# The right factor and the band output in DRAM: row, channel, column against channel, row, column

## What is computed

```python
xn = _ln(group_norm(x))                                   # 32 channels
left  = (xn @ Wl + bl) * mask * sigmoid(xn @ Wlg + blg)   # 64 channels
right = (xn @ Wr + br) * mask * sigmoid(xn @ Wrg + brg)   # 64 channels
out_gate = sigmoid(xn @ Wog + bog)
# band: out[i, k, h] = sum over |d| <= 4 of left[i + d, i, h] * right[i + d, k, h]
out = _ln(_banded_ingoing(left, right, 4)) * out_gate
x = x + out @ Wo + bo
```

## Time and profile before

| | us |
|---|---|
| median of 3 runs (3795.11 to 3798.96) | 3797.58 |
| the profiled execution | 3818.71 |
| its span, first to last instruction | 3816.9 |
| of it the three layers | about 0 to 1842 |
| of it the fourth layer | about 1842 to 3817 |
| TensorE busy | 2963.8 (78%) |
| VectorE busy | 2530.4 (66%) |
| DMA: packets, MB | 368217, 568.38 |

### The profile page before, as it was taken

The page is one execution under the profiler, slowest core; times in us unless marked ns, Lnnn a source line. Parts: engine busy times, 40 slices in busy tenths (PEclk is TensorE's granted clock), DMA queues, the critical chain, the costliest instruction groups (busy, mean ns, idle before and its releaser), DMA issues. The chain is left out here.

```text
span 3816.9 us, 37020 instructions
## 1 busy us (share of the span) xinstructions
PE 2963.8 (78%) x10962; PEld 864.5 (23%) x10962; DVE 2530.4 (66%) x2216; ACT 1906.5 (50%) x2326; POOL 1737.7 (46%) x964
## 2 busy tenths in 40 slices
PE   2685898695799596689168888888888888888886
PEld 0122322122222122222012222222222222222221
DVE  2243355143345143334159999999999999999998
ACT  0331344241244241235077677677776676676772
POOL 0110012110012120011147888878878878878876
PEclk9796998796899697899579999999999999999998
DMA  6866741766752656664747667667667676576674
GB/s 204 49 194 186 229 118 54 29 175 194 214 151 67 7 152 216 204 185 120 129 98 169 151 154 172 150 159 170 146 164 167 143 170 161 145 169 159 144 178 109
DMA packets 368217, 568.38 MB, mean 149 GB/s; under 512 B 144552, under 2 KB 247024, under 8 KB 367088
## 3 DMA queue, kind: packets, MB, share of 16 engines
q1 hardware_dynamic: 297216, 537.94, 55.3%
q10 hardware_dynamic: 70896, 29.14, 7.7%
HBM read 421.14 MB, written 145.80 MB: 149 GB/s over the span
## 5 line engine op out<-in xcount | busy, mean ns | idle before, releaser
L483 POOL TENSOR_TENSOR m_hs<-m_hs,m_cs 128x1024 f32<-128x1024 f32 x512 | 1205.6, 2360 | 347.4 <-DVE m_hs L457 347.4
L457 DVE TENSOR_TENSOR_SCAN m_hs<-m_da,m_pb 128x1024 f32<-128x1024 f32 x512 | 1170.9, 2287 | 33.2 <-ACT m_da L409 6.5
L303 PE MATMUL m_pb<-m_dtx,m_spread 64*128 64x512 f32 x2048 | 600.5, 652 | 219.0 <-DVE m_hs L457 218.4
L409 ACT ACTIVATE m_da<-m_dtb,m_a_neg 128x1020 f32<-128x1020 f32 x512 | 579.4, 1143 | 290.1 <-DMA m_dtb<-dt_rows 215.8
L452 DVE TENSOR_TENSOR m_pb<-m_pb,m_bs 128x1024 f32<-128x1024 f32 x512 | 620.6, 1212 | 34.9 <-PE m_pb L303 34.3
L1317 POOL TENSOR_TENSOR t_xc<-t_xc,t_xn 128x512 f32<-128x512 f32 x96 | 121.4, 1265 | 1112.2 <-DVE t_xn L1271 1112.2
L286 PE MATMUL m_py<-m_hs,m_gather 128*64 128x512 f32 x2048 | 566.6, 632 | 59.5 <-POOL m_hs L483 59.4
L1258 DVE TENSOR_TENSOR t_vwin<-t_bank,t_mask_k 128x512 f32<-128x512 f32 x204 | 140.4, 691 | 397.8 <-PE t_bank L968 274.3
L1314 POOL TENSOR_TENSOR t_sq<-t_xn 128x512 f32<-128x512 f32 x96 | 99.7, 1039 | 504.7 <-ACT t_xn L1163 504.7
L968 PE MATMUL t_bank<-t_rwin,t_lwin 128*128 128x256 f32 x816 | 244.7, 438 | 92.1 <-DVE t_vwin L1258 72.3
L303 PEld LDWEIGHTS m_pb<-m_dtx,m_spread 64*128 64x128 f32 x2048 | 168.2, 189 | 619.3 <-DVE m_hs L457 544.5
(11 more groups left out here) (144 smaller groups left out, 3649.0 us busy)
## 6 DMA issues: line engine op xcount, KB each, us to landing
m_dtb<-dt_rows SPq DMA_DIRECT2D x512, 512.0 KB, 6.1
right_factor<-t_tile SPq DMA_DIRECT2D x384, 128.0 KB, 2.7
t_rwin<-right_factor SPq DMA_DIRECT2D x96, 512.0 KB, 6.2
t_tile<-band_out SPq DMA_DIRECT2D x384, 128.0 KB, 3.0
t_lwin<-band_factor SPq DMA_DIRECT2D x96, 272.0 KB, 4.2
band_out<-t_vwin SPq DMA_DIRECT2D x48, 496.0 KB
band_out<-t_vwin SPq DMA_DIRECT2D x48, 480.0 KB
dt_rows<-m_dt ACTq DMA_DIRECT2D x64, 256.0 KB, 3.3
```

The costliest lines, as they stand in the source:

```text
L303: m = nc.tensor.matmul(pb[s % 2][:, half(n)], spread[rows, dg, :], dtx[par][rows, half(q)], start=True, stop=True)
L409: nc.scalar.activation(da[:, s % DA_RING, :, 1:T], dtb[s % DTB_RING][:, :].rearrange("p (r t) -> p r t", t=T)[:, :, 1:T], ACT.Exp, scale=a ...
L457: nc.vector.tensor_tensor_scan(hs[:, s % H_RING, :], da[:, s % DA_RING, :, :].rearrange("p r t -> p (r t)"), pb[s % 2][:, :], 0.0, ALU.mul ...
L483: nc.gpsimd.tensor_tensor(hs[:, s % H_RING, :], hs[:, s % H_RING, :], cs[q][:, :], ALU.mult).then_inc(hc_ready, 1)
```

## The change

`r_dram` and `v_dram` are declared as (channel, row, column) in place of (row, channel, column), and each DMA that touches them is written for it. What is computed, the order of all work, the waits and the sizes of all transfers stay the same. One channel's two image rows lie side by side now, so stores of L806 and loads of L830 are one piece of 2 KB a partition where they were two of 1 KB. Four channels of one row lie 256 KB apart now, so window loads and stores are four pieces of 1 KB a partition where they were one of 4 KB.

```diff
--- before.py
+++ after.py
@@ -803,9 +803,8 @@
                         slot = at[l, "r", n, p]
                         for hs in range(2):
                             row = first_row(n, 2 * p + (hs ^ n % 2))
-                            sp.dma_start(r_dram[row:row + 2, :, :].rearrange("r h k -> h r k"),
-                                         tile[HID * hs:HID * hs + HID, slot, :].rearrange("h (r k) -> h r k", r=2)
-                                         ).then_inc(tile_stored[slot], 16)
+                            sp.dma_start(r_dram[:, row:row + 2, :].rearrange("h r k -> h (r k)"),
+                                         tile[HID * hs:HID * hs + HID, slot, :]).then_inc(tile_stored[slot], 16)
 
                 def right_stored(l, n):
                     for slot in range(T_RING):
@@ -827,8 +826,8 @@
                         tile_free(sp, key)
                         for hs in range(2):
                             row = first_row(n, 2 * p + (hs ^ p))
-                            sp.dma_start(tile[HID * hs:HID * hs + HID, slot, :].rearrange("h (r k) -> h r k", r=2),
-                                         v_dram[row:row + 2, :, :].rearrange("r h k -> h r k")).then_inc(tile_loaded[slot], 16)
+                            sp.dma_start(tile[HID * hs:HID * hs + HID, slot, :],
+                                         v_dram[:, row:row + 2, :].rearrange("h r k -> h (r k)")).then_inc(tile_loaded[slot], 16)
 
                 def load_window(l, q):
                     slot = at[l, "chunk", q]
@@ -845,8 +844,8 @@
                         row = w_ * WIN_B
                         sp.dma_start(lwin[:, slot, :], band_dram[w_, :, HC * hc:HC * hc + HC, :].rearrange("j h i -> j (h i)")
                                      ).then_inc(win_loaded[slot], 16)
-                        sp.dma_start(rwin[:, slot, :], r_dram[row:row + P, HC * hc:HC * hc + HC, :].rearrange("j h k -> j (h k)")
-                                     ).then_inc(win_loaded[slot], 16)
+                        sp.dma_start(rwin[:, slot, :].rearrange("j (h k) -> j h k", h=HC),
+                                     r_dram[HC * hc:HC * hc + HC, row:row + P, :].rearrange("h j k -> j h k")).then_inc(win_loaded[slot], 16)
                     else:
                         c0 = HC * (q - 32)
                         for c in range(HC):
@@ -854,9 +853,8 @@
                             sp.dma_start(lwin[:, slot, o:o + P].rearrange("p (h i) -> p h i", h=8),
                                          corner_dram[:, c0 + c, :, BAND:BAND + 16]).then_inc(win_loaded[slot], 16)
                         for hg in range(8):
-                            sp.dma_start(rwin[16 * hg:16 * hg + 16, slot, :],
-                                         r_dram[ROW_C:ROWS, 8 * hg + c0:8 * hg + c0 + HC, :].rearrange("j h k -> j (h k)")
-                                         ).then_inc(win_loaded[slot], 16)
+                            sp.dma_start(rwin[16 * hg:16 * hg + 16, slot, :].rearrange("j (h k) -> j h k", h=HC),
+                                         r_dram[8 * hg + c0:8 * hg + c0 + HC, ROW_C:ROWS, :].rearrange("h j k -> j h k")).then_inc(win_loaded[slot], 16)
 
                 def store_window(l, q):
                     slot = at[l, "chunk", q]
@@ -867,13 +865,13 @@
                         w_, hc = divmod(q, 16)
                         lo, hi = (0, P - BAND) if w_ == 0 else (BAND, P - BAND)
                         row = w_ * WIN_B
-                        sp.dma_start(v_dram[row + lo:row + hi, HC * hc:HC * hc + HC, :].rearrange("j h k -> j (h k)"),
-                                     vwin[lo:hi, slot, :]).then_inc(win_stored[slot], 16)
+                        sp.dma_start(v_dram[HC * hc:HC * hc + HC, row + lo:row + hi, :].rearrange("h j k -> j h k"),
+                                     vwin[lo:hi, slot, :].rearrange("j (h k) -> j h k", h=HC)).then_inc(win_stored[slot], 16)
                     else:
                         c0 = HC * (q - 32)
                         for hg in range(8):
-                            sp.dma_start(v_dram[ROW_C + BAND:ROWS, 8 * hg + c0:8 * hg + c0 + HC, :].rearrange("j h k -> j (h k)"),
-                                         vwin[16 * hg + BAND:16 * hg + 16, slot, :]).then_inc(win_stored[slot], 16)
+                            sp.dma_start(v_dram[8 * hg + c0:8 * hg + c0 + HC, ROW_C + BAND:ROWS, :].rearrange("h j k -> j h k"),
+                                         vwin[16 * hg + BAND:16 * hg + 16, slot, :].rearrange("j (h k) -> j h k", h=HC)).then_inc(win_stored[slot], 16)
 
                 def store_x(n):
                     sp.wait_ge(x_done, 2 * UNITS * (LAYERS - 1) + n + 1)
@@ -1403,8 +1401,8 @@
          for n, t in arrays.items()}
     band_dram = nc.dram_tensor("band_factor", (2, P, HID, LROW), F32, kind="Internal").ap()
     corner_dram = nc.dram_tensor("corner_factor", (P, 8, 8, 24), F32, kind="Internal").ap()
-    r_dram = nc.dram_tensor("right_factor", (ROWS, HID, COLS), F32, kind="Internal").ap()
-    v_dram = nc.dram_tensor("band_out", (ROWS, HID, COLS), F32, kind="Internal").ap()
+    r_dram = nc.dram_tensor("right_factor", (HID, ROWS, COLS), F32, kind="Internal").ap()
+    v_dram = nc.dram_tensor("band_out", (HID, ROWS, COLS), F32, kind="Internal").ap()
     x3 = nc.dram_tensor("x_layer3", (C, ROWS, COLS), F32, kind="Internal").ap()
     out = nc.dram_tensor("out_cm", (C, COLS, ROWS), F32, kind="ExternalOutput").ap()
     dt_dram = nc.dram_tensor("dt_rows", (2, 2, 64, 2, 512), F32, kind="Internal").ap()
```

## The result

| | us |
|---|---|
| before, median of 5 runs (3795.11 to 3801.88) | 3798.96 |
| after, median of 5 runs (3817.3 to 3836.57) | 3820.86 |
| ratio after to before | 1.0066, 95% interval 1.0044 to 1.0089 |
| after, the profiled execution | 3826.36 |
| its span | 3824.6 |

The time went the way that was forecast and lies in the range, but the kernel lost 22 us by the medians (25 by the ratio) and not 52. The spans of the two profiled executions differ by 7.7 us only. At the two changes of layer, which the change doesn't touch, the profile of before took 126.8 and 129.1 us from the last band load to the first store of the right factor, where every other profile of this study took 122 to 124.

What follows compares the result with a forecast made beforehand. Four DMA engines, filled by 124-partition window stores, were taken to bound the first window. Terms of 41 (short pieces), 5 (second window) and 6 (SyncE's issue) made +52 us: 3797.6 + 52 = 3850, 8 in 10 range 3795 to 3905.

Steps and rivals of the forecast that it cites:

- What bounds the kernel: First window: 124-partition stores use engines 0 to 3 only, full for 105 of 109 us; what lengthens their work lengthens the layer.
- the stretch: First window, 844.7 to 953.6 us, third window store to first band load: 109 us, forecast to become 122.
- spread: Window stores of 124 x 4 pieces divide over 16 engines, VectorE's ring waits mostly vanish: 3705 us; 5%.
- The price of short pieces: First window on four engines: four 1 KB pieces cost 188 ns against 159; with right factor +13.7 us a layer, three layers +41.
- The windows before the third store: Two stores and six right windows before the stretch, where engines have gaps: put at nothing, at most 3.2 us a layer.
- The second window: 985 to 1065 us, stores on 15 engines: pieces ahead of band loads grow, +1.6 us a layer; three layers +5.
- the corner: SyncE issues without pause there; issue changes make +3.8 us, half may show: +2 a layer, three layers +6.
- SyncE's issue: DMA with two dimensions of pieces issues in 608 ns, with one in 420 to 433; the change turns these round: +6.
- Far apart: Window pieces at a 256 KB stride: the stride costs nothing that shows, 67 against 69 ns a KB.
- same: Four engines gain on the right factor what windows lose, or the 29 ns lie beside work: 3798 us; 8%.
- faster by size: Rival slightly faster: small pieces cost nothing at the four engines and 2 KB loads come earlier each cycle: 3783 us; 7%.
- much slower: 1 KB window pieces cost 69 ns, by stride, port or held SyncE, +51 us a layer: 3960 us; 14%.

Runs made afterwards that it cites:

- the kernel with near, aligned rows: Kernel before, order row, channel, column kept, but a 256 B gap after each channel's row of the band output: 3823.97 us, ratio 1.0065.

## Why the prediction was right in direction and wrong in size

**What bounds the kernel: right.** Four engines of 16 are full from the third store on, because a store has 124 partitions. In the stretch of the kernel before, the trace has fewer than four packets under way for 0.1 of 108.9 us, and in that of the changed kernel for 1.0 of 115.1. The edit from 124 to 128 rows took 116 us off, and the stretch without any change to the layout went from 109.5 to 75.6 us. The rival "spread" (the new pattern divides over 16 engines) did not come true: 97 GB/s with a store alone is four engines' rate. Its price was too low: with 16 engines at a store the changed kernel ran 120 us faster than before, and not 93.

**The price of short pieces: the step that failed.** The term that was mis-sized is the price of four 1 KB pieces in place of one of 4 KB. I took 47 ns for 1 KB and 159 for 4 KB, +29 ns a window row. The rate of the four engines says otherwise: 4 engines x 2 us / 51 pieces = 157 ns for 4 KB and 42.2 for 1 KB, so 4 x 42.2 = 169 against 157: +12. The row that carried my figure said 25.9% where four engines are 25%. I divided busy time by pieces. The trace gives each packet of that row: 60 pieces of 46 ns, three of 159 and eight signals of 9. So 47 was, within 1 ns, how long a piece lasts, and that is not what it costs, since the next one starts 4 ns before it ends; for pieces of 4 KB the overlap is 2 ns. Four times 4.8 less 2 is the 17 ns by which +29 was too much. The same row would have warned: 4 engines x 0.8 us are 3.2 us, and (3.2 - 3 x 0.157) / 60 = 45.5 ns with the signals at nothing. The 29 ns in 188 by which the prediction saw the Trainium skill's rule of 512 B ("DMA: Bandwidth & Descriptors", section Specifications) fail are 12 in 169 by the rates. That rule still does not hold, but by less than half as much.

With 12 ns the term is 434 x 12 = 5.2, window loads 80 x 12 = 1.0, the right factor's stores -1.2: 5.0 us a layer. Measured: 6.1 more with both arrays changed (109.5 to 115.6), 7.3 with the band output alone, -1.2 with the right factor alone. Three layers: 18 us where I had 41. VectorE's wait, put at 165 us, and the stretch, put at 122, came to 140.9 and 115.1 for the same reason. The sum of one engine's work, 105 us in the prediction, is 103 by the rates; by the packets under way the engines are busy for all 109, so some 6 us are in no term of the sum. Pieces that are dearer when all 16 engines work may be it: over the whole stretch the 1 KB pieces of the kernel before last 70 ns in the mean and not 46.

**The rest of the stretches.** The windows before the third store, put at nothing with 3.2 us a layer as a bound, took 2.0 more: +6. The second window, put at +5, and the corner, put at +6, took nothing: 151.5 and 151.3 us from the first band load to the last corner issue. The sum is 18 + 6 = 24, against 22 by the medians and 25 by the ratio.

**SyncE's issue: wrong in its reason.** I read L806's 608 ns against 420 to 433 as the price of a second dimension and expected it to change places. In the profile after (duration ns min/median/max):

```profile
L806 SPq DMA_DIRECT2D right_factor<-t_tile x384: 445/597/6688, 154.8 to 1554.4; - x192
```

```profile
L847 SPq DMA_DIRECT2D t_rwin<-right_factor x96: 422/435/1474, 222.5 to 1661.5; - x96
```

```profile
L856 SPq DMA_DIRECT2D t_rwin<-right_factor x48: 425/426/1102, 494.0 to 1689.5; - x48
```

```profile
L868 SPq DMA_DIRECT2D band_out<-t_vwin x96: 248/452/5134, 235.2 to 1690.0; - x96
```

L847 and L856 have two dimensions of pieces now and take 435 and 426 ns, as with one. L806 has one in place of two: its shortest issue fell from 574 to 445 ns, and in the trace that is the first of each group of four, but the median is 597 where it was 608, and L829, the loads of the band output, do the same. So the number of dimensions does not do what my term says: a DMA that gains one pays nothing, and one that loses one saves 0.13 us in one issue of four. What holds the other three was not tested. The corner's issues, L856 and the stores of L873 (364 ns before, 372 after), got no longer to speak of, and this is why the corner cost nothing.

**Far apart, same, faster by size.** That the stride of 256 KB costs nothing was read from the stores to x_layer3 and is now shown by the kernel with near, aligned rows: 115.4 against 116.8 us in the stretch (band output alone in the new layout). The rival "much slower" falls with it. The rival "same", a piece's cost hidden or none, falls by the ratio's interval, and so does "slightly faster". The gain by larger pieces of the right factor does not stand out of the spread: -1.2 us a layer in the stretch, window loads included, and -1 us (-5 to +2) for the kernel.

## What to carry to other kernels

Look for the DMA that uses few of the engines, as the store of 124 partitions does here with four where one of 128 takes 16: what else lies on those few waits behind it, while the mean DMA share (0.63 to 0.66) looks harmless. Such a store is where a layout's price is paid: four engines paid 12 ns for each 4 KB cut into four, some 18 of the 22 to 25 us that the kernel lost, and 128 rows in place of 124 took away the loss and 116 us besides. Take the price of a piece from the rate at which a known number of engines passes pieces over a few us in which nothing else runs, and in more than one place, not from busy time over count. Where a layout leaves gaps, try one that keeps piece starts on multiples of 256 B; here it was worth some 12 us.

## What was not expected of the hardware

A store of many pieces on few engines holds the issuing sequencer. SyncE's issues in the changed kernel, by time (start us, us, line, count):

```profile
904.08 5.20 SPq L868 DMA_DIRECT2D band_out<-t_vwin  x2
909.33 6.71 SPq L806 DMA_DIRECT2D right_factor<-t_tile  x3
```

The first of the two stores took 0.4 us to issue, the second 4.7, and the first of the three issues behind it 5.3 (the longest of L868 is 5.1 us, that of L806 6.7). Before, a pair at 915.03 took 3.18 us. Over the stretch SyncE's issues last 106 of 115 us, where they lasted 72 of 109. It cost little that the stretch shows, since fewer than four packets were under way for 1.0 us of it, but a load that must leave early should not stand behind such a store.

Consecutive short pieces overlap on an engine: 45.9 ns long and 42.2 apart at 1 KB, 0.287 x 32 / 340 = 27.0 long and 23.5 apart at 512 B. A busy share above the share of the engines at work is the sign of it.
